# The rows of ones under the keys by a DMA, and the half maxima joined by an instruction with one operand

## What is computed

```
h    = group_norm(x)                               # 256 channels, 1024 positions
q, k, v = split(qkv_w @ h + qkv_b)                 # 8 heads of 32 channels
s    = einsum('bhdq,bhdk->bhqk', q, k) * 32**-0.5  # 1024 x 1024 scores for each head
p    = softmax(s, axis=-1)                         # subtract the row's maximum, exp, divide by the sum
o    = einsum('bhqk,bhdk->bhqd', p, v)
x    = x + proj_w @ o + proj_b
```

## Time and profile before

| | us |
|---|---|
| three runs | 5702.43, 5707.20, 5717.48 |
| median | 5707.20 |
| the profiled execution, device time | 5702.98 |
| its span, first to last instruction | 5701.3 |
| mean granted TensorE clock in it | 0.848 of full |

### The profile page before, as it was taken

One profiled execution on the slowest core, in us unless ns is written; L12 is line 12 of the kernel. 1 busy time (PEld: TensorE's weight loads), 2 busy tenths in 40 slices (PEclk: granted clock), 3 DMA queues, 4 the chain that ended last, 5 costly groups with the idle time before them and its releaser, 6 DMA issues.

```text
span 5701.3 us, 44537 instructions
## 1 busy us (share of the span) xinstructions
PE 4237.7 (74%) x16298; PEld 1839.3 (32%) x16298; DVE 3892.5 (68%) x4825; ACT 2109.0 (37%) x2575; POOL 2221.3 (39%) x721
## 2 busy tenths in 40 slices
PE   4678866788658886588865878658786587855878
PEld 2233422333224332243322433223332243322433
DVE  7764788647886478764787646876468774686746
ACT  3233442334423344233442435324253242542424
POOL 4541435414454044540445404444045440454404
PEclk7689977899778997699977999769897798976999
DMA  0020100211002100021000220002200012000120
GB/s 34 0 52 16 30 8 4 49 24 22 8 8 45 33 13 8 8 45 36 10 8 8 45 45 1 8 9 44 45 1 8 18 35 45 8 1 18 27 45 8
DMA packets 58845, 125.24 MB, mean 22 GB/s; under 512 B 14713, under 2 KB 16889, under 8 KB 58370
## 3 DMA queue, kind: packets, MB, share of 16 engines
q1 hardware_dynamic: 58626, 122.39, 9.2%
HBM read 12.23 MB, written 8.39 MB: 4 GB/s over the span
## 4 chain that ended last, share of the span: by engine, by line
PE 44%; DVE 34%; issue 9%; ACT 5%; SPq 4%; POOL 2%; DMA 2%; DVEq 0%; ACTq 0%; POOLq 0%
DVE mx L947 10%; PE PS L1288 8%; PE PS L1246 7%; PE PS L1080 6%; PE PS L1336 6%; PE PS L1370 4%; DVE work L839 3%; PE PS L1139 2%; DVE work L841 2%; PE PS L1180 2%; DVE mboth L954 2%; SPq L284 2%; PE PS L1297 2%; DVE small L714 2%; SPq L293 1%
## 5 line engine op out<-in xcount | busy, mean ns | idle before, releaser
L947 DVE TENSOR_REDUCE mx<-PS 128x1 f32<-128x512 f32 x2048 | 1336.3, 686 | 419.5 <-PE PS L1246 415.2
L617 ACT ACTIVATE PT<-PS 128x1024 f32<-128x1024 f32 x1024 | 1007.4, 1022 | 706.5 <-PE PS L1336 679.1
L1246 PE MATMUL PS<-KS,QS 96*128 96x512 f32 x2048 | 894.7, 479 | 194.6 <-DMA KS<-piece 84.6
L423 POOL TENSOR_TENSOR piece<-PT 128x2048 f32<-128x2048 f32 x48 | 219.9, 4581 | 2000.2 <-ACT PT L617 2000.2
L423 POOL TENSOR_TENSOR piece<-piece,PT 128x2048 f32<-128x2048 f32 x192 | 877.4, 4570 | 61.7 <-ACT PT L617 50.4
L399 POOL TENSOR_TENSOR work<-work,Crep 128x1024 f32<-128x1024 f32 x256 | 615.7, 2406 | 434.2 <-DVE work L839 240.9
L1336 PE MATMUL PS<-QS,KS 98*128 98x512 f32 x2048 | 685.2, 427 | 50.3 <-DMA QS<-nm 32.2
L1246 PEld LDWEIGHTS PS<-KS,QS 96*128 96x128 f32 x2048 | 376.7, 197 | 814.9 <-DVE mx L947 575.1
L1288 PE MATMUL PS<-PT,Vt 128*32 128x512 f32 x4096 | 554.1, 613 | 7.6 <-ACT PT L617 7.6
L1180 PE MATMUL PS<-dstk,sel 128*128 128x512 f32 (+1 forms) x640 | 313.1, 564 | 320.6 <-DVE work L841 133.5
L1180 PE MATMUL PS<-ustk,sel 128*128 128x512 f32 (+1 forms) x640 | 329.4, 587 | 285.4 <-DVE work L824 155.0
(11 more groups left out here) (212 smaller groups left out, 5556.3 us busy)
## 6 DMA issues: line engine op xcount, KB each, us to landing
QS<-piece SPq DMA_DIRECT2D x384, 128.0 KB, 2.4
KS<-piece SPq DMA_DIRECT2D x384, 128.0 KB, 2.4
xin<-x SPq DMA_DIRECT2D x8, 1024.0 KB
out<-xr SPq DMA_DIRECT2D x8, 1024.0 KB, 4.0
W<-wpack SPq DMA_DIRECT2D x2, 1024.0 KB
QS<-nm SPq DMA_DIRECT2D x128, 8.0 KB, 1.9
W<-wpack SPq DMA_DIRECT2D x1, 576.0 KB
W<-wpack SPq DMA_DIRECT2D x2, 256.0 KB
```

Source lines behind the costliest of these rows:

```text
L423: pool.tensor_tensor(total, first, PT[:, i % 3, :, :], ALU.add).then_inc(sum_pool.sem, 1)
L617: act.activation(PT[:, i % 3, 2 * pr:2 * pr + 2, :], PS[:, 2 + 2 * pr:4 + 2 * pr, :], ACT.Exp, scale=SCALE).then_inc(p_sb.sem, 1)
L947: dve.tensor_reduce(mx[:, cc, at:at + 1], PS[:, row_slot(n, cc), :], AX.X, ALU.max).then_inc(r_max.sem, 1)
L1246: pe.matmul(PS[:, row_slot(n, cc), :], QS[0:kd, c, h, q * P:q * P + P], KS[0:kd, h, cc * N:cc * N + N], start=True, stop=True).then_inc(r_ ...
```

## The change

Two edits. (1) The fill by GpSimd is gone. SP issues one DMA for each sample, right behind the load of the next input, that writes rows 96 and 97 of KS from a constant tile of ones (`ones32`, 32 columns, read again and again); TensorE's wait is for the DMA's 16 instead of GpSimd's 1. (2) `mx` is laid out with the two halves of a row side by side, and the join is a reduction over these two (one operand) instead of a maximum of two operands.

```diff
@@ -156,7 +156,7 @@
-            mx = so("mx", [P, NC, PHASE_ROWS])
+            mx = so("mx", [P, PHASE_ROWS, NC])
@@ -230,7 +230,7 @@
-        ones_in = sig("ones_in", 1)
+        ones_in = sig("ones_in", 16)
@@ -308,6 +308,8 @@
                     sp.dma_start(xin[0:1, 0, 0:N], x_v[b][0:1, 0, 0:N]).then_inc(xin_here.sem, 16)
+                ones = ones32[96:98, None, 0:32].broadcast_to((2, HEADS * L // 32, 32))
+                sp.dma_start(KS[96:98, :, :].rearrange("p h (r w) -> p (h r) w", w=32).bitcast(F32), ones).then_inc(ones_in.sem, 16)
                 attention(b, 0)
@@ -403,10 +405,6 @@
-                pool.wait_ge(*x_new(b, 4))
-                one = ones32[96:98, 0:1].broadcast_to((2, HEADS * L))
-                pool.tensor_tensor(KS[96:98, :, :].rearrange("p h n -> p (h n)"), one, one,
-                                   ALU.mult).then_inc(ones_in.sem, 1)
                 for a in range(2):
@@ -944,14 +942,14 @@
-                    dve.tensor_reduce(mx[:, cc, at:at + 1], PS[:, row_slot(n, cc), :], AX.X,
+                    dve.tensor_reduce(mx[:, at, cc:cc + 1], PS[:, row_slot(n, cc), :], AX.X,
                                       ALU.max).then_inc(r_max.sem, 1)
...
-                        dve.tensor_tensor(mboth[:, :], mx[:, 0, :], mx[:, 1, :], ALU.max).then_inc(m_both.sem, 1)
+                        dve.tensor_reduce(mboth[:, :], mx[:, :, :], AX.X, ALU.max).then_inc(m_both.sem, 1)
@@ -1272,7 +1270,7 @@
-                pe.wait_ge(*ones_in(b, 1))
+                pe.wait_ge(*ones_in(b, 16))
```

## The result

| | before | after |
|---|---|---|
| median of the runs, us | 5704.8 (4 runs) | 5574.8 (4 runs) |
| lowest to highest | 5700.9 to 5717.5 | 5570.5 to 5588.0 |
| ratio, 95% interval | | 0.9768 (0.9746 to 0.9791) |
| the profiled execution | 5702.98 | 5587.96 |
| its mean granted clock | 0.848 | 0.848 |

The change makes the kernel 130 us faster, 2.3%. Later, beside the experiments on two chips, the same kernel stood at 0.9797 (0.9782 to 0.9811) and 0.9776 (0.9760 to 0.9793) of the kernel before, 118 and 131 us less. Of all runs in this document two, both of e9_join_pad3 and one of them its profiled one, came out disturbed (5820 and 7798 us) and are not counted.

The account below looks back on a forecast made before the run. Bound: a long relay between TensorE and VectorE, neither full. Sum -93.7 + 0 - 33.1 + 0.3 = -126.5 us from the 5707.2 us median gives 5580.7, predicted as 5581 us; range 5557 to 5605.

Parts of the forecast that it names:

- Part 1: Group norm ahead of attention: without GpSimd's fill, L714 falls from 11.88 to 0.17 us, 93.7 us less over 8 samples.
- Who locks whom: VectorE instructions with two SBUF operands wait until the GpSimd instruction begun before ends; those with one SBUF operand do not.
- the cold start: First eight projections L1080 start at the 1.2 GHz level and take 5.39 us, expected the same after the change.
- My rival of a warm start: TensorE's clock stays at 2.4 GHz over the shortened norm, 14.8 us more gained, 5566 us; chance 0.09.
- Part 2: Ones by DMA on SP's queue, done before the first stacking transfer: 0 us, range up to +19 us.
- Part 3: Join of the half maxima as a one-operand reduction of 0.2 us, not waiting for GpSimd: 33.1 us less.
- The 0.65 us at the change of phase 0 to 1: Value products behind the transpose start 0.65 us earlier, at 382.35 instead of 383.00, with ScalarE as next bound.
- The extra at the last change: Between phases 2 and 3 the nm transfer and L1336 come 0.77 us earlier, 16 times, 12.3 us.
- The whole wait: TensorE's whole wait for the transpose comes back, 48 x 1.08 = 51.8 us instead of 33.1, 5562 us; chance 0.08.
- the reduction held up by GpSimd: The new join waits for GpSimd as well, so only the norm's 93.7 us come, 5613.5 us; chance 0.03.
- the blocked queue: The ones' DMA blocks the stacking transfers behind it, making the kernel slower, for example 5754 us; chance 0.03.
- The clock: TensorE's granted clock after the shortened norm, left out of the sum: 14.8 us more gained or as much lost.

Follow-up runs that it names:

- e9_join_pad3: The changed kernel with three unused VectorE reductions of 512 columns ahead of the join in phases 1 to 3; 5613.9 and 5615.2 us, ratio 0.9828 to the kernel before.
- e1: The kernel before with only the join changed to a reduction over pairs, GpSimd still filling the ones; 5674.6 us against 5711.0, ratio 0.9940.
- e3: The kernel before with the new join, and GpSimd filling the ones by a memset instead of a product that reads; 5590.7 us against 5711.0, ratio 0.9793.
- e2: The kernel before with only the ones moved to the DMA, the join keeping its two operands; 5625.5 us, ratio 0.9853.
- e7: The changed kernel with five unused TensorE products in the group norm ahead of attention 0; 5565.7 us against 5585.5 for the changed kernel, ratio 0.9760 to the kernel before.
- e5: The changed kernel as it is, run again as point of comparison on the first chip; 5585.5 us, ratio 0.9797 to the kernel before.
- e12: The changed kernel as it is, run again as point of comparison on another chip; 5582.9 us, ratio 0.9776 to the kernel before.
- e11: The changed kernel with unused TensorE products fitted to the gaps in the group norms alone; 5534.0 us against 5582.9, ratio 0.9687 to the kernel before.

## Why the prediction was right

The forecast was 126.5 us less and 5581 us; it came to 130 us less and 5574.8, inside the range of 5557 to 5605. The mechanism held in both parts. That the total came within 4 us is partly luck: the same kernel gave 118, 130 and 131 us in three measurements, and part 1 by itself was 10 us below its term. Point by point:

- **Who locks whom.** Right, and settled by e1 to e3. What the prediction read from three VectorE rows beside the fill held in every run. It did not foresee that a GpSimd fill that only writes holds up another VectorE instruction (e3); no row of before showed that, and the change doesn't meet it.
- **Part 1, 93.7 us.** The norm is 11.9 us shorter, as forecast (11.7); the other 0.21 us is L1069, which took 0.59 us at a granted clock of 0.50 and, as L1067, takes 0.38 at 1.00. But part 1 alone brought 84 us (e2). The term left out is the projections behind the norm: 6.22 - 5.39 = 0.83 us in 8 samples is 7 us back. I had named the cold start and kept its length equal; it got longer. The 4 us that are left are within e2's interval. My rival of a warm start did not come by itself, and e7 shows what it would have been worth.
- **Part 2, 0 us.** Right. I took 25 ns a packet and two engines; measured are 22.6 ns and two. SP's queue carried this before:

```profile
q1 hardware_dynamic: 58626, 122.39, 9.2%
```

It carries 62738 - 58626 = 4112 packets more in 8 transfers, 514 each, the 512 pieces and two more. In the first sample the two engines are done by 296, 5 us ahead of the first stacking transfer at 301.44, and the wait for the keys is 5.22 us (5.29 before). The rule on the number of engines that the prediction cites from the Trainium skill ("DMA: Bandwidth & Descriptors", section on why a DMA increments its semaphore by 16 and not by 1) gives two here, and the trace agrees: a share of 0.10 to 0.12. That transfers below 512 bytes fall short of line rate, which the prediction cites from the same page of the Trainium skill, agrees too: 128 bytes in 22.6 ns are 5.7 GB/s for an engine, where stacking had 13.7. It stays hidden and costs this kernel nothing; whether a read-modify-write is behind it no run shows.
- **Part 3, 33.1 us.** 34 us in e1. The 0.65 us at the change of phase 0 to 1 is exact. The extra at the last change was mis-sized twice over. The rows of before beside those of the earlier trace rows, and after:

```profile
454.28 1.02 ACT L617 ACTIVATE PT<-PS 128x1024 f32<-128x1024 f32 x1
```

```profile
434.58 1.94 ACT L615 ACTIVATE PT<-PS 128x1024 f32<-128x1024 f32 x2 [2.46 <-PE PS L1334]
...
439.46 1.20 PE L1334 MATMUL PS<-QS,KS 98*128 98x512 f32 x4
...
440.59 1.01 ACT L615 ACTIVATE PT<-PS 128x1024 f32<-128x1024 f32 x1
```

The scores L1334 start 439.46 - 434.58 = 4.88 us after the exponentials instead of 5.81, 0.93 us earlier and not 0.77, and the wait for the nm transfer that the prediction expected to stay there is gone. But the exponentials of the next phase start 6.01 us after those of the last step instead of 6.66, so only 0.65 goes on. ScalarE's logarithm and exponential of the sums stand ahead of them. By that the term is 48 x 0.65 = 31.2 us.
- **The rivals.** The whole wait (52 us) is outside e1's interval; the reduction held up by GpSimd is out by 0.186 us in all 64; the blocked queue exists, but needed eight times as many packets for 5 us a sample.
- **The clock.** The prediction allowed 14.8 us either way; the changed kernel's own four runs lie between 5570.5 and 5588.0. The profiled one is 11.5 us short of the 126.5, and its trace shows where. Between the first projection and the first scores the sixteen heads take 279.8 us, 266.8 in the kernel before. 6.5 of these 13 us are the cold start of attention 0. The rest is in attention 1 of four samples, where the same 24 rows ran at the low level for a while (granted clock 0.58 from 2619 to 2623); first such a place, then one in a sample where the clock was 1.00:

```profile
2619.10 12.13 PE L1078 MATMUL PS<-xg,W 128*128 128x512 f32 x24 [2.24 <-ACT xg L565]
```

```profile
3313.09 10.54 PE L1078 MATMUL PS<-xg,W 128*128 128x512 f32 x24 [2.24 <-ACT xg L565]
```

Another 5.1 us are lost between the first scores and the transposes (422.7 us against 417.6), and some 6.6 are won elsewhere. In e5 two samples have the slow projections of attention 1, in e12 three, in the kernel before none. Why the clock falls there in some samples and not in others stays open.

The version that beats both is e11, at 0.9687 of the kernel before.

## What to carry to other kernels

Look for a tiny VectorE instruction with a long duration beside a GpSimd one: the shortest run of the same line says what it takes alone (not the median: three of four joins were locked), and the cure here was a form with one operand or a transfer in place of the GpSimd work. Then price it by the idle time of the engine that waits, less the next release behind it: 2 us a join were 1.08 us of idle time and 0.65 us of gain. After shortening a gap ahead of TensorE, look at the clock behind it.

## What the runs showed of the hardware that I had not expected

- A GpSimd memset of 2 x 8192 numbers takes 6.92 us, the product of two broadcast ones 13.84. The memset leaves a VectorE product of two SBUF operands alone (0.17 us) and holds up a VectorE scaling of 1024 columns (3.63 us instead of 0.81).
- SBUF to SBUF, a DMA packet of 128 bytes takes 22.6 ns on its engine and one of 16 bytes 8.1 ns.
- A transfer of 4096 packets ahead in the queue holds up the issue of the next one, 5.69 us instead of 0.60, and until it is nearly through no engine carries anything else (DMA share 0.12 against 0.95 behind it).
- Products with unused results in TensorE's idle time make the kernel 49 us faster in the norms; at the heads of the attentions as well they lose 22 us of that again.
